# Keys and values of all eight tile pairs moved behind the expert blocks, the delta's addition moved from GpSimd to VectorE, and the last stage woven into the last tiles

## The reference, cut to what matters

```python
x = x + _L0_xattn_ref(_layernorm(x), ctx, ...)            # linear attention
x = x + _L0_ffn_ref(_layernorm(x), ...)                   # experts, routed and shared
x = x + _L1_xattn_ref(_layernorm(x), ctx, mask, ...)      # softmax attention on ctx:
#   q = proj(hs, Wq, bq); k = proj(ctx, Wk, bk); v = proj(ctx, Wv, bv)
#   scores = clip(q k / 4), masked; probs = softmax(scores)
#   delta = rs * ((probs v) @ Wo.T + bo)
#   delta = (delta - mu) / sqrt(var + eps) * ln_gamma + ln_beta
x = x + _L1_ffn_ref(_layernorm(x), W0, bias0, W1, bias1)  # fp16 halves, exact gelu
```

## Time and profile before

| | |
|---|---|
| median of three runs | 482.74 us (481.18 to 487.18) |
| the profiled execution | 482.49 us |
| its span, first to last instruction | 480.4 us |
| PE busy | 416.4 us, 87% of the span |
| DVE, ACT, POOL busy | 304.1, 249.8 and 221.8 us |
| mean granted clock of PE | 0.925 |

### The profile page before, as it was taken

One profiled execution on the slowest core, in us unless ns is written; L12 is line 12 of the kernel. 1 busy time (PEld: TensorE's weight loads), 2 busy tenths in 40 slices (PEclk: granted clock), 3 DMA queues, 4 the chain that ended last, 5 costly groups with the idle time before them and its releaser, 6 DMA issues.

```text
span 480.4 us, 10413 instructions
## 1 busy us (share of the span) xinstructions
PE 416.4 (87%) x3368; PEld 373.8 (78%) x3368; DVE 304.1 (63%) x871; ACT 249.8 (52%) x575; POOL 221.8 (46%) x379
## 2 busy tenths in 40 slices
PE   2899999999988997999788393999799987799995
PEld 1777888888766897999788382888698876799995
DVE  4488788778665796654435384888557782556642
ACT  4475765764522314685667263565556545435360
POOL 4355553885645702152226777775344463521200
PEclk9899998998988999999899876999679997599999
DMA  8621222125011442676535313111000000001011
GB/s 273 200 68 48 59 54 65 55 78 188 29 44 68 165 153 68 194 236 213 166 111 165 93 57 88 56 51 36 5 2 1 2 1 0 1 25 44 22 45 44
DMA packets 31731, 39.30 MB, mean 82 GB/s; under 512 B 4289, under 2 KB 29122, under 8 KB 31682
## 3 DMA queue, kind: packets, MB, share of 16 engines
q1 hardware_dynamic: 28610, 30.29, 20.5%
q0 software_dynamic: 3072, 8.39, 5.2%
HBM read 25.03 MB, written 13.63 MB: 80 GB/s over the span
## 4 chain that ended last, share of the span: by engine, by line
PE 54%; DVE 15%; POOL 9%; issue 8%; ACT 7%; DMA 5%; SPq 1%; DVEq 0%; ACTq 0%; POOLq 0%
PE PS L339 10%; PE PS L340 8%; PE PS L341 8%; PE PS L2151 7%; PE PS L2254 7%; DVE arena_f L1664 2%; PE PS L2168 2%; DMA x<-in_x 2%; DMA raw<-in_w_l 2%; PE PS L1896 2%; POOL raw L710 2%; ACT raw L1006 2%; POOL rows_early L710 2%; PE PS L1822 2%; SPq L491 1%
## 5 line engine op out<-in xcount | busy, mean ns | idle before, releaser
L1044 ACT ACTIVATE arena_f<-PS,cols 128x256 f16<-128x256 f32 x64 | 26.7, 470 | 29.8 <-PE PS L2151 28.0
L463 POOL TENSOR_TENSOR w1l<-raw,w1h 128x384 fp32r<-128x384 f32 x16 | 15.0, 936 | 54.4 <-ACT w1h L450 54.4
L2151 PE MATMUL PS<-arena_r,w1h 128*128 128x256 f32 x128 | 35.5, 310 | 3.2 <-ACT arena_r L1055 2.5
L339 PE MATMUL PS<-wfh,arena_r 128*128 x120 | 35.6, 297 | 2.9 <-issue 1.4
L339 PE MATMUL PS<-w0h,arena_r 128*128 128x256 f32 (+1 forms) x96 | 36.7, 382 | 0.0
L2151 PE MATMUL PS<-arena_r,w1l 128*128 128x256 f32 x128 | 34.7, 304 | 0.0
L340 PE MATMUL PS<-wfl,arena_r 128*128 x120 | 33.9, 282 | 0.0
L341 PE MATMUL PS<-wfh,arena_r 128*128 x120 | 33.7, 281 | 0.0
L340 PE MATMUL PS<-w0l,arena_r 128*128 128x256 f32 (+1 forms) x96 | 32.7, 341 | 0.0
L341 PE MATMUL PS<-w0h,arena_r 128*128 128x256 f32 (+1 forms) x96 | 32.5, 338 | 0.0
L2254 PE MATMUL PS<-w1h,arena_r 128*128 128x256 f32 x128 | 31.6, 287 | 0.9 <-DVE arena_f L1750 0.9
(11 more groups left out here) (296 smaller groups left out, 1513.3 us busy)
## 6 DMA issues: line engine op xcount, KB each, us to landing
arena_f<-xs_rows SPq DMA_DIRECT2D x40, 128.0 KB, 2.2
ys_rows<-raw SPq DMA_DIRECT2D x20, 256.0 KB, 2.3
raw<-in_w_ffn SPq DMA_DIRECT2D x16, 241.0 KB, 2.6
raw<-in_w_l SPq DMA_DIRECT2D x16, 192.0 KB, 3.2
ctx_raw<-in_ctxT SPq DMA_DIRECT2D x16, 128.0 KB, 2.1
out<-arena_f SPq DMA_DIRECT2D x8, 256.0 KB, 2.1
x<-in_x SPq DMA_DIRECT2D x1, 1792.0 KB, 10.1
raw<-in_w_l SPq DMA_DIRECT2D x2, 512.0 KB, 5.0
```

The lines of the kernel that those rows point to most:

```text
L339: nc.tensor.matmul(out_ap, lh, rh, start=first, stop=False)
L463: last = nc.gpsimd.tensor_tensor(w1l[:, to], raw[:, r * FFN_CHUNK:r * FFN_CHUNK + L1_CHUNK], w1h[:, to].bitcast(F32), ALU.subtract)
L1044: nc.scalar.activation(md16[:, r, n, :], PS[:, M_H + n // 2, (n % 2) * D:(n % 2 + 1) * D], ACT.Gelu, bias=cols[:, 2 * KC + n:2 * KC + n + ...
L2151: last = nc.tensor.matmul(PS[:, M_H + n // 2, (n % 2) * D:(n % 2 + 1) * D], m0w[w][:, c, n * P:(n + 1) * P], mX[r][:, c, :], start=c + w = ...
```

## The change

Keys and values: none is left between the blocks. PE makes the keys of pair 0 in iteration 20 and of pair 1 in iteration 21 of the block loop (where only transposes and the last down products remain), then values 0 and 1, then pairs 2 to 7. POOL clears pairs 0, 1, 4, 5; ACT clears 6 and 7 (a copy of zeros and two of ones), DVE 2 and 3 (memsets). POOL issues six gathers ahead of the slots in place of nine. `add_delta` goes to DVE. The transposes of the first group stand in slot 14, all of `ffn_hidden(0)` in slot 16, `halves_T(1)` in slot 17 and the output of group 0 in slot 18. The loops of the last stage are written out; in it PE's order is now `halves_T(g)`, `ffn_hidden(g)`, output of g-1. In `slot2` ACT does the queries ahead of the probabilities.

```diff
-LOAD_CTX_AT, CTX_AT, KEYS_AT = (4, 12, 14, 19), (6, 8, 16, 20), (12, 16)
+LOAD_CTX_AT, CTX_AT = (4, 12, 14), (6, 8)
+ZERO_ACT, ZERO_DVE = (6, 7), (2, 3)
-KEYS_BANK, VALUES_BANK = (7, 7, 7, 2, 7, 2, 7, 2), (7, 7, 6, 1, 6, 1, 6, 1)
+X_K, X_V = (7, 2), (6, 1)
...
# SP, behind the last two stores
-            for p in range(5, CPAIRS):
+            for p in range(4, CPAIRS):
                 load_ctx_pair(p)
...
# POOL
-            def add_delta(t):
-                pool.wait_ge(S2["beta"], t + 1)
-                pool.wait_ge(S2["scaled"], t + 1)
-                nc.gpsimd.tensor_tensor(x[:, t, :], x[:, t, :], dn[:, t % 2, :], ALU.add).then_inc(x_done[2], 1)
...
             pool.wait_ge(E["gu"], 2 * BPAIRS)
-            for p in range(2, 6):
-                values_setup(p)
+            values_setup(4, 2)
+            ctx_pair_lo(2)
+            values_setup(5, 3)
+            ctx_pair_lo(3)
...
-            gather(0)
-            gather(1)
-            values_setup(6)
-            gather(2)
+            for t in range(3):
+                gather(t)
             joint_rstd(0)
             gather(3)
-            values_setup(7)
             joint_rstd(1)
             gather(4)
             joint_rstd(2)
-            for t in range(5, 9):
-                gather(t)
+            gather(5)
             def slot2(s):
                 if s.at + 3 < TILES + JOIN:
                     joint_rstd(s.at + 3)
...
-                if tile := s.tile(-6):
-                    add_delta(tile[0])
-                if tile := s.tile(9):
+                if tile := s.tile(6):
                     gather(tile[0])
...
# ACT, behind the blocks (values_zeroed: a Copy of 128x1088 zeros, two of 64x32 ones)
+            keys(1)
+            ctx_pair_hi(2)
+            ctx_pair_hi(3)
             keys(2)
             ctx_pair_hi(4)
             keys(3)
             ctx_pair_hi(5)
             keys(4)
+            ctx_pair_hi(6)
+            act.wait_ge(E["y"], BPAIRS)
+            values_zeroed(6, 0)
+            keys(5)
+            ctx_pair_hi(7)
             norm_x(0)
-            ctx_pair_hi(6)
-            keys(5)
+            values_zeroed(7, 1)
+            keys(6)
...
# DVE, behind the blocks (values_zeroed: memsets of 128x1088 and twice 64x32)
+            values_zeroed(2, 0)
+            values(0)
+            values(1)
+            values_zeroed(3, 1)
             values(2)
             ctx_pair_lo(4)
             values(3)
             ctx_pair_lo(5)
-            entering(0)
             values(4)
             ctx_pair_lo(6)
+            entering(0)
+            values(5)
+            ctx_pair_lo(7)
             entering(1)
-            values(5)
+            values(6)
...
+            def add_delta(t):
+                dve.wait_ge(S2["scaled"], t + 1)
+                dve.wait_ge(S2["beta"], t + 1)
+                nc.vector.tensor_tensor(x[:, t, :], x[:, t, :], dn[:, t % 2, :], ALU.add).then_inc(x_done[2], 1)
# DVE, slot2
                 if leaving:
                     d_aggr(leaving[0])
+                if done:
+                    gamma(done[0])
+                if s.is_at(TILES):
+                    ffn_halves(0, range(2))
...
+                if done:
+                    add_delta(done[0])
                 if past:
                     normalise(past[0])
+                if s.is_at(TILES):
+                    ffn_halves(0, range(2, 4))
...
# PE, block loop
+                if j == BPAIRS:
+                    keys(0)
                 if 1 <= j <= BPAIRS:
                     block_hT(j - 1)
-                if j in KEYS_AT:
-                    keys(KEYS_AT.index(j))
-                if j - 2 in KEYS_AT:
-                    values(KEYS_AT.index(j - 2))
                 if j == BPAIRS + 1:
-                    keys(2)
+                    keys(1)
...
# PE, slot2 and behind it
+                if s.is_at(TILES):
+                    pe.wait_ge(S2["clipped"], 2 * TILES)
+                    ffn_hidden(0)
                 if tile := s.tile(-1):
                     weighted_values(tile[0])
+                if s.is_at(TILES + 2):
+                    ffn_out(0)
                 if tile := s.tile(-3):
                     output(tile[0])
...
-                if s.is_at(TILES - 1):
+                if s.is_at(TILES - 2):
                     pe.wait_ge(setup_v, 6)
                     halves_T(0)
...
                 if s.is_at(TILES + 1):
-                    ffn_hidden(0, 0, EARLY[4:])
+                    halves_T(1)
             each_slot(0, TILES + 2, slot2)
+            ffn_hidden(1)
+            for g in range(2, GROUPS):
+                halves_T(g)
+                ffn_hidden(g)
+                ffn_out(g - 1)
+            ffn_out(GROUPS - 1)
```

More of the change, by code:

```diff
@@ L43 @@
 GROUPS = TILES // PER_GROUP
-EARLY, LATE = range(6), range(6, NFF)
 VC = P + HPC
@@ L107, in tile @@
         return t, (self.ring + ahead) % 2
-    def next(self, ahead, over=2):
-        t = self.at + ahead
-        if isinstance(t, int) and not 0 <= t < self.count + over:
-            return None
-        return t, (self.ring + ahead) % 2
     def is_at(self, at):
         return isinstance(self.at, int) and self.at == at
-def slots(eng, count, first, last, body, low=4):
-    high = (count - 1) // 2 * 2
-    for s in range(first, low):
-        body(Slot(s, s % 2, count))
-    with eng.Fori(low // 2, high // 2) as i:
-        body(Slot(i * 2, 0, count, i))
-        body(Slot(i * 2 + 1, 1, count, i))
-    for s in range(high, last + 1):
-        body(Slot(s, s % 2, count))
 def each_slot(first, last, body):
@@ L773, in slot2 @@
                     add_beta(tile[0])
-            each_slot(0, TILES + 5, slot2)
-            def slot3(s):
-                if tile := s.tile(2):
-                    for k in range(2):
-                        ln_rstd_step(pool, tile[0] * 2 + k, k)
-            slots(pool, GROUPS, 0, GROUPS - 3, slot3, low=2)
+            each_slot(0, TILES + 4, slot2)
+            for t in range(4, TILES):
+                ln_rstd_step(pool, t)
         @block.scalar
@@ L1557, in _ @@
                     output_bias()
-                if j - 3 in KEYS_AT:
-                    values(KEYS_AT.index(j - 3))
             def combine(t):
@@ L1762, in _ @@
+            add_delta(TILES - 2)
+            ffn_halves(1)
+            gamma(TILES - 1)
+            add_delta(TILES - 1)
+            ln_group(3)
+            for g in range(2, GROUPS):
+                ffn_halves(g)
+                if g + 2 < GROUPS:
+                    ln_group(g + 2)
+                ffn_out(g - 1)
+            ffn_out(GROUPS - 1)
         @block.tensor
@@ L2055, in values @@
                     for c in range(KC):
-                        last = product(PS[:, VALUES_BANK[p], r * D:(r + 1) * D], [w[:, c, r * P:(r + 1) * P] for w in parts],
+                        last = product(PS[:, X_V[p % 2], r * D:(r + 1) * D], [w[:, c, r * P:(r + 1) * P] for w in parts],
                                        [w[:, c, :] for w in v1w], c == 0, c == KC - 1)
@@ L2110, in normed_T @@
                 last.then_inc(xT_psum, 1)
-            values(2)
-            for p in range(3, 6):
+            for p in range(2):
+                values(p)
+            for p in range(2, 7):
                 keys(p)
@@ L2117, in _ @@
             normed_T(0)
-            keys(6)
-            values(6)
+            keys(7)
             normed_T(1)
-            keys(7)
+            pair_queries(0)
             values(7)
-            pair_queries(0)
-            normed_T(2)
             def halves_T(g):
-                first = isinstance(g, int) and g == 0
-                if first:
+                if g == 0:
                     pe.wait_ge(S2["q_ready"], 4 * CPAIRS)
-                else:
-                    after(pe, S3["x_ready"], g, 1, per=2)
-                for k in range(2):
-                    after(pe, xn_ready, g, per=2, base=LN_BASE[3], extra=k - 1)
+                elif g == 1:
+                    pe.wait_ge(S2["cn_ready"], TILES)
+                else:
+                    pe.wait_ge(S3["x_ready"], 2 * g)
+                for t in (2 * g, 2 * g + 1):
+                    pe.wait_ge(xn_ready, LN_BASE[3] + t + 1)
```

340 lines of the change are left out of this document (163 added, 177 removed).

## The result

Median of four runs after the change: 455.02 us (450.97 to 458.13), before 481.96 us on the same chip. 27 us less by the medians, 5.6%; the ratio of the comparison is 0.939, 95% interval [0.928, 0.950]. The forecast was 456. The profiled execution took 453.87 us, span 452.1. In some executions of this and later kernels the stretch up to the 10th block_out, which no edit touches, ran up to 12 us longer, for a reason that stays open; therefore the experiments are read mainly by the distances inside their traces, from the 10th block_out on.

What follows compares the result with a forecast made beforehand. PE, busy 87% of the span, was taken as the bound, with pauses and half-clock stretches to win. The parts, -10 - 4 - 8.3 - 4 = -26.3, took 482.5 to 456 us, range 446 to 466.

Steps and rivals of the forecast that it cites:

- Part 1: Blocks without keys and values: block_out 9 to 19 in 27.4 to 30.0 us against 38.85, taken as -10.
- Part 2: From the blocks to the first slots: the gain comes one slot later, with fewer gathers ahead; -4, bounds -7 and +3.
- the sign that I named against it: Part 2 would be wrong if the first scores came more than 32 us past the last block.
- the walk: Part 2, steps timed from the last block's end: values(6) near +19, normed_T(0) near +18.5, first scores about +30.5.
- Part 3: Tile stage: with add_delta on DVE the stall between scores(7) and scores(9) falls away; -8.3, at worst -4.
- what is late next is PE itself: Part 3: with the stall gone, PE itself sets the pace, two slots taking 11.14 us.
- Part 4: Last stage reordered: 8 us less, but 4.5 more for a wait ahead of six hidden products; -4, bounds -8 and +1.
- 8 us less: Part 4, end of halves_T(0) to hidden(2): 31.3 us becomes 23.3, with two holes and 2 us for half clock.
- Rival (b): Behind the blocks and in the last stage, holes close and the clock stays at 2.4 GHz: 448 us; chance 0.17.
- (a): DVE becomes the bound of the tile stage, three two-input SBUF ops taking 0.75 us more per slot: 471 us; chance 0.07.
- (c): Removing POOL's addition only uncovers the next waiter; half of part 3, all of part 4 lost: 464.5 us; chance 0.15.
- (d): Pairs behind the blocks run one step at a time, 8.9 us a pair: 492 us, slower; chance 0.03.

Runs made afterwards that it cites:

- e4: Changed kernel with the blocks and the stretch up to the first slot as before the change: 470.36 us, ratio 0.971.
- e12: Changed kernel with e5's last stage, halves_T(0) behind scores(15), clears of pairs 6, 7 on POOL, first two entering tiles one step earlier on DVE: 454.21 us.
- e2: Changed kernel with the delta's addition back on POOL, gamma still ahead of the sums on DVE: 465.36 us, ratio 0.963.
- e3: Changed kernel with the next group's halves_T again behind ffn_hidden in the last stage, from group 2: 453.08 us, ratio 0.932.
- e5: As e3, but with the output of group 1 ahead of the halves of group 3: 465.97 us, ratio 0.960.
- e7: Changed kernel with the addition of the attention's delta to x left out on DVE: 465.61 us.
- e1: Kernel before with only the delta's addition moved to DVE and gamma ahead of the sums: 475.29 us, ratio 0.984.
- e8: Changed kernel with the delta's addition made twice on DVE, the first time into a spare tile: 475.96 us, ratio 0.980.
- e6: Changed kernel with the clears of pairs 6 and 7 moved from ACT to POOL, behind the third gather: 466.11 us, ratio 0.959.
- e9: Changed kernel once more, unaltered: 471.17 us (459.77 to 472.21).
- e10: Kernel before once more, unaltered: 485.77 us, ratio 1.002.

## Why the prediction was right

**Part 1** (-10; measured -9.2; the 1.6 ahead of the cut is within what executions differ by). The blocks take 29.6 us, inside the 27.4 to 30.0 of the prediction, near its upper end. The reason holds: keys and values between blocks cost not 1.4 us a set but the waits between them, and e4, which has them back, takes 39.6. The size is less sure than one trace suggests: the ten traces with the new block loop take from 28.3 (e12) to 32.1 us (e2), the four with the old one 38.9 to 39.9.

**Part 2** (-4; measured -3.8). Right in place: the first scores didn't gain, the second did. But the sign that I named against it came up, the first scores 32.5 us behind the last block and not the 30.5 of the walk. The step that failed is "Norm 0 is then near +18, normed_T(0) near +18.5": normed_T(0) began at 268.72, +20.4. The walk's sizes weren't at fault. e2 and e3 have the same code up to there, and in them normed_T(0) began at +18.86 and the first scores at +31.05 and +30.79. What the walk lacked are pauses that come in some executions and not in others. ACT's split of ctx of pair 4 (L931), in the changed kernel and in e3, 8.24 and 7.36 us behind the end of their last blocks (248.37 and 250.64):

```profile
256.61 0.63 ACT L931 ACTIVATE arena_r<-ctx_raw 128x512 fp32r<-128x512 f32 x1 [0.69 <-issue]
```

```profile
258.00 0.64 ACT L931 ACTIVATE arena_r<-ctx_raw 128x512 fp32r<-128x512 f32 x1
```

By the next pair's keys the changed kernel was 1.5 us behind e3, and it stayed so up to normed_T(0). "issue" is time for which the profile shows no reason, so the cause stays open. The saving up to scores(1), with the same code, lies between 1.4 us (e5, e7) and 5.6 (e3); that the first trace has 3.8 where I said 4 is in part luck. Behind normed_T(0) the second one waited 2.20 us more for DVE's low part of the first, and there e12's earlier entering is worth 1.3 to 1.7 us. My clears were close: a memset took 0.96 us on DVE where I had 1.1. Of the 6.35 us ahead of the fourth normed_T, 1.02 are left.

**Part 3** (-8.3; measured -6.2, and -7.8 with halves_T(0) counted in part 4). The mechanism held, as e1 and e2 show, and alone it is worth 8.1 us by times and 8.7 by the trace of e1. The term that was mis-sized is "what is late next is PE itself": the 11.14 us that I took for PE's own work are 10.96 and a wait of 0.18 for DVE's low part. In the changed kernel this wait is 0.46, 0.89, 1.07 and 0.71 us in the pairs from scores(5) to (13), which take 11.42, 11.85, 12.04 and 11.67. The kernel before had such waits, too (3.7 us in all from 240 us on), and so has e1 (0.18, 0.85, 0.60, 0.59). DVE fills 17.4 of 20 us in the windows from 320 to 340, 4.8 of a slot, as I had worked out. But that it fits doesn't put it in time. The group of these low parts on DVE (300 to 360 us; busy, mean ns, then idle before them and by whom):

```profile
L1590 DVE TENSOR_TENSOR arena_r<-PS,arena_r 128x256 fp32r<-128x256 f32 x10 | 4.2, 420 | 6.8 <-ACT arena_r L1054 6.8
```

DVE stood idle for 6.8 us ahead of ten of them, for ACT's high parts. Late next is thus a chain in which all the small engines take part (DVE's moments, POOL's joint_rstd, ACT's norm and high part, DVE's low part). That an instruction more on DVE lengthens the wait, e8 shows; that one less doesn't shorten it, e7. Which link is late in which slot is not shown.

**Part 4** (-4; measured -7.6, and -6.0 with halves_T(0); 3.7 to 4.9 by e4 and e1). The price of the added wait was right as a pause, 0.75 us six times; with its restart it is 8.88 - 7.97 = 0.91 us a group, 5.5 us. The term that was too small is the "8 us less". It stands for the way from the end of slot 15 to hidden(2), 31.3 us before (392.39 to 423.71). Now it is 21.1 us (369.57 to 390.71), with the first of the six pauses; without it 20.4, where I had 23.3. So 10.9 us went, not 8. I had left two holes of 3.7 us together; the waits there are 1.5 us in four (0.35, 0.29, 0.36, 0.49). I had left 2 us for half clock, and every window is at 1.00. Against this, the work is some 18.9 us and not 17.6. Of the 10.9 us, 4.7 are waits that the traces show: before, they were 1.75, 1.23, 0.66 and 2.51. (The prediction's four largest waits leave out the 1.23, at 406.81, for the 0.66.) The other 6 us or so are half clock and pauses too short to be listed. Three windows in a row of the kernel before had lost clock, 390 to 400 and 400 to 410 us besides the 0.58 of the earlier trace rows:

```profile
390.00:400.00 10.00, 7.70 (x67) 7.02 (x66) 5.32 (x17) 5.87 (x14) 6.23 (x14) 0.83 0.00 0
400.00:410.00 10.00, 7.16 (x33) 6.28 (x34) 4.46 (x15) 3.38 (x9) 3.79 (x9) 0.74 0.01 2
```

Together (0.17 + 0.26 + 0.42) x 10 = 8.5 us of full clock, part of it inside pauses, where it costs nothing. The gain isn't safe: e4, e6 and e9, with the same last stage, have a window below 0.90 between 390 and 400 us and take 84.1 to 84.2 us from scores(15) on, 1.5 to 1.6 more than the first trace. Rival (b)'s condition was met in the tile and the last stage of the first trace, not in the handover.

**The rivals.** (a) is out: the addition took 0.36 us eight times of eight between 300 and 360 us. A group of DVE's instructions shows that its neighbour does stretch at times:

```profile
L1669 DVE TENSOR_TENSOR arena_f<-arena_f,rows 128x256 f32<-128x256 f32 x8 | 4.1, 517 | 0.0
...
L1674 DVE TENSOR_TENSOR x<-x,arena_f 128x256 f32<-128x256 f32 x8 | 2.9, 361 | 0.0
```

Gamma's mean is 0.52 us, 0.16 above the addition of the same shape, a fifth of what (a) priced. Six of the eight took 0.39 us and two 0.90, and both of these overlapped POOL's addition of beta (L720, also 128x256), which then took 0.98 and 0.97 us in place of 0.73:

```profile
321.82 0.90 DVE L1669 TENSOR_TENSOR arena_f<-arena_f,rows 128x256 f32<-128x256 f32 x1
```

```profile
322.33 0.98 POOL L720 TENSOR_TENSOR x<-x,rows 128x256 f32<-128x256 f32 x1
```

The row of 1.11 lay beside POOL's addition of beta, too (335.41 to 336.14). The rule of the Trainium skill (SBUF — State Buffer, "Who interferes with whom") says that a DVE instruction with two SBUF inputs contends with a GpSimd instruction that reads SBUF, and the trace agrees. The addition's even 0.36 us doesn't speak against it: none of the 16 additions of the changed kernel overlapped one of beta. DVE's mixing steps took 0.46 to 0.49 us clear of it and up to 0.98 beside it. So contention is there, but only in the few slots where the two meet, and (a) had priced it for three instructions in every slot.

(c) is out by e1 and e4, though in mild form it is the waits of 0.5 to 1.1 us a pair above. (d) is out: no set of keys or values waits more than 1.7 us behind the blocks in the first trace.

**What is luck.** The sum is better than its parts: part 3 fell 0.5 us short, part 4 was 2 us too cautious, part 1 lacked 0.8 us, and 1.6 us came from a stretch for which I had 0. The hit within 1 us is luck besides, since e9, the same kernel, has its median at 471 us, outside the range. What the experiments support is the sign, the mechanisms, and a gain of 22.6 to 26.8 us behind the 10th block_out.

## What to carry to other kernels

Look for loops through a slow engine's queue: here an addition of 0.72 us on POOL cost 8 us, since it waited for DVE with the next tile's norm queued behind it. When an instruction is moved, place it by what must come first behind it on its new engine; a share of busy time only says whether it can fit. In this kernel the transposes of the next group are best put behind the current long product and not directly ahead of the product that needs their copy, but only as far ahead as the engine that makes their input has come. And cut two traces where the work is the same on both sides: a piece that was moved over a cut changes the size of two parts and not the sum.

## What had not been expected of the hardware

In the changed kernel's first trace the tile and the last stages ran at 1.00 in every window with six pauses of 0.75 us in them. That isn't sure to come again: e9, the same kernel, has a window at 0.83 between 390 and 400 us, and takes 1.6 us longer from scores(15) on.

The same program, over code that was not edited, reached its 10th block_out at 218 us in one execution and at 230 in another, with more of PE's time at 1.2 GHz (0.66 against 0.83 between 150 and 160 us). And behind the blocks, the first scores of one and the same code came 30.8 to 34.7 us after the last block, while the kernel before and e1, e4 and e10 with its code all have 31.14 or 31.15. Here the distance between two near events in a trace was worth more for a verdict than a difference of two totals, and only when the same distance had been seen in several traces of the same code.
